# Layer 1 of an attention kernel: scores as three single-pass split products over four row tiles, with the work of a row redistributed and reordered

## What is computed

```python
bias = jnp.einsum('nijz,zh->nhij', pair_repr, bias_proj)[:, None]
gate = jax.nn.sigmoid(msa_repr @ gate_proj).reshape(bs, s, r, head, c)
q, k, v = jnp.split(msa_repr @ qkv_proj, 3, axis=-1)
...
sim = jnp.einsum('nsqhc,nskhc->nshqk', q, k) * scale
sim = jax.nn.softmax(sim, axis=-1)
sim = sim + bias
attend = jnp.einsum('nshqk,nskhc->nsqhc', sim, v) * gate
out = attend.reshape(bs, s, r, cm) @ out_proj
```

## Time and profile before

| | us |
|---|---|
| median of 3 runs (range) | 4940.08 (4938.53 to 4940.24) |
| the profiled execution | 4934.87 |
| its span, first to last instruction | 4932.9 |
| TensorE busy | 4651.9 |
| VectorE busy | 4024.4 |
| ScalarE busy | 3523.2 |
| GpSimd busy | 3464.3 |
| TensorE clock granted, mean | 0.973 of full |

### The profile page before, as it was taken

How to read it: one execution, slowest core, us unless ns; L and a number is a source line. 1 busy time by engine, 2 the same in 40 slices (tenths; PEclk the granted TensorE clock), 3 DMA queues, 4 the chain that set the end, 5 groups by cost and what they waited for, 6 DMA issues and landing times. The chain is left out here.

```text
span 4932.9 us, 149816 instructions
## 1 busy us (share of the span) xinstructions
PE 4651.9 (94%) x44087; PEld 3925.1 (80%) x44087; DVE 4024.4 (82%) x12910; ACT 3523.2 (71%) x11216; POOL 3464.3 (70%) x5926
## 2 busy tenths in 40 slices
PE   4663999999999999999999989999999999999999
PEld 2332888888888888888888868888888888888887
DVE  4445888888888988888888868888888888888887
ACT  2222888888888888888888866666666666666665
POOL 3332888888888888888888846666666666666665
PEclk8776999999999999999999989999999999999999
DMA  8995111111111111111111101111111111111111
GB/s 330 356 355 173 53 51 60 56 54 60 51 60 52 59 56 55 60 51 60 51 59 52 59 29 53 51 51 51 47 49 51 51 51 51 51 51 51 51 50 40
DMA packets 237352, 382.70 MB, mean 78 GB/s; under 512 B 18756, under 2 KB 156616, under 8 KB 224968
## 3 DMA queue, kind: packets, MB, share of 16 engines
q1 hardware_dynamic: 237256, 381.63, 23.0%
HBM read 309.21 MB, written 72.35 MB: 77 GB/s over the span
## 5 line engine op out<-in xcount | busy, mean ns | idle before, releaser
L1337 POOL TENSOR_SCALAR l_probs<-l_probs,l_inv 128x256 f32<-128x256 f32 x2048 | 943.2, 478 | 735.7 <-DVE l_inv L1242 730.2
L1161 ACT ACTIVATE l_probs<-bank,l_neg_max 128x256 f32<-128x256 f32 x2048 | 947.0, 481 | 486.2 <-DVE l_neg_max L1236 486.2
L563 POOL TENSOR_SCALAR l_probs<-l_probs,l_inv 128x256 f32<-128x256 f32 x2048 | 947.5, 476 | 279.6 <-DVE l_inv L814 279.6
L732 ACT ACTIVATE l_probs<-l_probs,l_neg_max 128x256 f32<-128x256 f32 x2048 | 1020.8, 518 | 10.3 <-DVE l_neg_max L806 10.0
L806 DVE CUSTOM_DVE_ANT_0 l_probs<-bank,bias 128x256 f32<-128x256 f32 x2048 | 779.6, 418 | 202.8 <-PE bank L673 199.1
L1236 DVE TENSOR_REDUCE l_neg_max<-bank 128x2 f32<-128x512 f32 x1024 | 646.6, 684 | 92.3 <-PE bank L1070 92.3
L1249 DVE TENSOR_TENSOR l_probs_t<-bank,bias 128x512 f32<-128x512 f32 x1024 | 674.6, 682 | 35.4 <-PE bank L1080 5.4
L673 PE MATMUL bank<-ident,l_probs 128*128 128x128 f32 x4096 | 629.5, 276 | 8.4 <-DVE l_probs_t L828 7.3
L1080 PE MATMUL bank<-ident,l_probs 128*128 128x128 f32 x4096 | 531.7, 273 | 3.2 <-POOL l_probs L1337 1.6
L673 PEld LDWEIGHTS bank<-ident,l_probs 128*128 128x128 f32 x4096 | 463.7, 141 | 44.7 <-issue 8.4
L686 PE MATMUL bank<-l_probs_t,l_v 128*64 128x256 f32 x4096 | 498.5, 385 | 0.2 <-issue 0.2
(11 more groups left out here) (196 smaller groups left out, 14011.6 us busy)
## 6 DMA issues: line engine op xcount, KB each, us to landing
fp_x<-in_x_dram SPq DMA_DIRECT2D x32, 1024.0 KB, 6.9
fp_ln_w<-in_L_conv_ln_w_dram SPq DMA_DIRECT2D x32, 1024.0 KB, 8.9
fp_ln_b<-in_L_conv_ln_b_dram SPq DMA_DIRECT2D x32, 1024.0 KB, 10.8
fp_pair<-in_L_conv_pair_repr_dram SPq DMA_DIRECT2D x32, 1024.0 KB, 13.4
l_x<-in_x_dram SPq DMA_DIRECT2D x128, 256.0 KB, 2.9
l_ln_w<-in_L_conv_ln_w_dram SPq DMA_DIRECT2D x128, 256.0 KB, 3.4
l_ln_b<-in_L_conv_ln_b_dram SPq DMA_DIRECT2D x128, 256.0 KB, 3.5
x<-l_y SPq DMA_DIRECT2D x128, 256.0 KB, 2.0
```

Source lines behind the costliest of these rows:

```text
L563: last = nc.gpsimd.tensor_scalar(probs[:, h, c], probs[:, h, c], inv[:, h, c:c + 1], 1.0, ALU.mult, ALU.mult)
L732: last = nc.scalar.activation(probs[:, h, c], probs[:, h, c], ACT.Exp, bias=neg_max[:, h, c:c + 1], scale=-1.0, accum_out=total[:, h, c:c ...
L1161: last = nc.scalar.activation(probs[:, h, c], b_s[h % 4][:, c * W:(c + 1) * W], ACT.Exp, bias=neg_max[:, h, c:c + 1], accum_out=total[:, h ...
L1337: last = nc.gpsimd.tensor_scalar(probs[:, h, c], probs[:, h, c], inv[:, h, c:c + 1], 1.0, ALU.mult, ALU.mult)
```

## The change

It touches `layer1` and the helper that writes out the loops.

- `scores` makes three single-pass products (high by high, high by low, low by high) for each head, 24 matmuls a quad in place of 8, accumulated in the same banks, on the same four row tiles.
- q and k are stored as high and low parts. ACT's copies make the high parts. `queries_low` on DVE reads q's bank again for the low part. For k, ACT copies the bank a second time (`keys_whole`), and `keys_low` on POOL subtracts.
- `group_norm` goes from DVE to ACT, as scale and bias by channel; the bias (-mean x 1/deviation) is made once ahead of the loop.
- `turn` runs five rows ahead (`AHEAD` 5, before 3), loads seven; quad 1's scores, half of the transposes and `attend` of a row come one step later than before. Every engine's order is new, and the bank hand-over waits of PE are written anew. `b_t` is chosen by the head's parity.
- The last two turns of each loop are written out (`ends=2`) instead of one.

The diff, cut to its core:

```diff
+    UNROLL, BUFS = 4, 4
+    AHEAD = 5
     QUADS = NH1 // 4
-    TURNS = (1, 0, 3, 2, 5, 4, 6, 7)
-    EXPS = (1, 2, 3, 0, 5, 4, 6, 7)
-    MAXIMA = (1, 2, 3, 0, 5, 4, 7, 6)
-    INVERSES = (1, 2, 3, 0, 5, 4, 6, 7)
-    DIVISIONS = (1, 3, 0, 2, 5, 4, 6, 7)
+    TURNS = (1, 2, 3, 0, 5, 4, 7, 6)
+    EXPS = (1, 2, 3, 0, 6, 5, 7, 4)
+    MAXIMA = (1, 2, 3, 0, 6, 7, 5, 4)
+    INVERSES = (1, 0, 2, 3, 6, 7, 5, 4)
+    DIVISIONS = (1, 2, 0, 3, 5, 4, 6, 7)
+    BIASED = (1, 2, 3, 0, 5, 4, 6, 7)
...
-        q = sb("q", [P, 2, HC, W])
-        kk_ = sb("k", [P, 2, HC, W])
+        q = [sb("q_high", [P, 2, HC, W], F32R), sb("q_low", [P, 2, HC, W], F32R)]
+        kk_ = [sb("k_high", [P, 2, HC, W], F32R), sb("k_low", [P, 2, HC, W], F32R)]
+        k_whole = sb("k_whole", [P, HC, W])
...
-            over_rows(engine, C0, UNROLL, row, ahead=AHEAD, behind=1)
+            over_rows(engine, C0, UNROLL, row, ahead=AHEAD, behind=1, ends=2)
...
-                if has(4):
-                    load(t, k + 4)
+                if has(7):
+                    load(t, k + 7)
...
             def turn(t, k):
-                s, i, tt = UNROLL * t + k, k % UNROLL, t + k // UNROLL
+                s, i, tt = UNROLL * t + k, k % BUFS, t + k // BUFS
                 pe.wait_ge(loaded[i], 16 * (tt + 1))
-                wait(pe, v_ready, s)
+                if exists(s - 3):
+                    pe.wait_ge(q_ready, s - 2)
+                elif exists(s - 4):
+                    pe.wait_ge(v_ready, s - 3)
+                elif exists(s - 1):
+                    pe.wait_ge(x_whole, s)
...
             def queries(t, k):
                 s = UNROLL * t + k
                 pe.wait_ge(x_ready, s + 1)
+                if exists(s - 1):
+                    pe.wait_ge(v_ready, s)
+                elif exists(s + 2):
+                    pe.wait_ge(x_whole, s + 3)
+                elif exists(s - 1):
+                    pe.wait_ge(q_ready, s)
...
             def keys(t, k):
                 s = UNROLL * t + k
                 pe.wait_ge(x_ready, s + 1)
-                if isinstance(s, int) and s < 3:
-                    wait(pe, g_ready, s)
-                    wait(pe, o_ready, s - 1)
-                else:
-                    pe.wait_ge(y_ready, s - 2)
+                if exists(s - 1):
+                    pe.wait_ge(g_ready, s)
+                elif exists(s - 3):
+                    pe.wait_ge(o_ready, s - 2)
+                elif exists(s - 4):
+                    pe.wait_ge(y_ready, s - 3)
+                elif exists(s - 1):
+                    pe.wait_ge(k_copied, s)
...
             def values(t, k):
                 s = UNROLL * t + k
-                pe.wait_ge(q_ready, s + 1)
+                pe.wait_ge(x_ready, s + 1)
+                if exists(s + 3):
+                    pe.wait_ge(x_whole, s + 4)
+                elif exists(s):
+                    pe.wait_ge(q_ready, s + 1)
+                elif exists(s - 1):
+                    pe.wait_ge(v_ready, s)
...
             def gates(t, k):
                 s = UNROLL * t + k
-                pe.wait_ge(k_ready, s + 1)
+                pe.wait_ge(x_ready, s + 1)
+                if exists(s - 2):
+                    pe.wait_ge(o_ready, s - 1)
+                elif exists(s - 3):
+                    pe.wait_ge(y_ready, s - 2)
+                elif exists(s):
+                    pe.wait_ge(k_copied, s + 1)
+                elif exists(s - 1):
+                    pe.wait_ge(g_ready, s)
...
                 for c in range(KC):
-                    for j in range(4):
-                        channels = slice(j * D1, (j + 1) * D1)
-                        last = nc.tensor.matmul(b_s[j][:, c * W:(c + 1) * W], q[channels, k % 2, quad, c * P:(c + 1) * P], kk_[channels, k % 2, quad],
-                                                start=True, stop=True, tile_position=(D1 * j, 0))
+                    for a, b in ((0, 0), (0, 1), (1, 0)):
+                        for j in range(4):
+                            channels = slice(j * D1, (j + 1) * D1)
+                            last = nc.tensor.matmul(b_s[j][:, c * W:(c + 1) * W], q[a][channels, k % 2, quad, c * P:(c + 1) * P],
+                                                    kk_[b][channels, k % 2, quad], start=a + b == 0, stop=a == 1, tile_position=(D1 * j, 0))
                 last.then_inc(s_mm[quad], 1)
 
...
             def transposes(t, k, h):
                 s = UNROLL * t + k
                 pe.wait_ge(p_ready, count(s, h, DIVISIONS))
-                wait(pe, t_ready, count(s, h, TURNS) - 2)
+                same = [g for g in TURNS if g % 2 == h % 2]
+                ahead = same[same.index(h) - 1]
+                wait(pe, t_ready, count(s if same.index(h) else s - 1, ahead, BIASED))
...
-                if inside(s + 1):
+                if exists(s - 1):
+                    pe.wait_ge(y_ready, s)
+                elif exists(s + 2):
+                    pe.wait_ge(k_copied, s + 3)
+                elif exists(s + 1):
                     pe.wait_ge(g_ready, s + 2)
-                else:
-                    pe.wait_ge(y_ready, s - 1)
+                elif exists(s - 1):
+                    pe.wait_ge(o_ready, s)
...
-                if inside(s + 1):
-                    pe.wait_ge(o_ready, s + 2)
-                else:
+                if exists(s + 3):
+                    pe.wait_ge(k_copied, s + 4)
+                elif exists(s + 2):
+                    pe.wait_ge(g_ready, s + 3)
+                elif exists(s):
+                    pe.wait_ge(o_ready, s + 1)
+                elif exists(s - 1):
                     pe.wait_ge(y_ready, s)
...
-                nc.scalar.activation(q[:, k % 2], b_xqv[:].rearrange("p (a c) -> p a c", a=HC), ACT.Copy).then_inc(q_ready, 1)
+                nc.scalar.activation(q[0][:, k % 2], b_xqv[:].rearrange("p (a c) -> p a c", a=HC), ACT.Copy).then_inc(q_high, 1)
...
-                nc.scalar.activation(kk_[:, k % 2], b_kgo[:].rearrange("p (a c) -> p a c", a=HC), ACT.Copy).then_inc(k_ready, 1)
+                nc.scalar.activation(kk_[0][:, k % 2], b_kgo[:].rearrange("p (a c) -> p a c", a=HC), ACT.Copy).then_inc(k_high, 1)
+
+            def keys_whole(t, k):
+                s = UNROLL * t + k
+                act.wait_ge(k_mm, s + 1)
+                wait(act, k_ready, s)
+                nc.scalar.activation(k_whole[:], b_kgo[:].rearrange("p (a c) -> p a c", a=HC), ACT.Copy).then_inc(k_copied, 1)
+
+            def group_norm(t, k):
+                s = UNROLL * t + k
+                act.wait_ge(x_mm, s + 1)
+                wait(act, x_ready, s - 1)
+                for c in range(HC):
+                    last = nc.scalar.activation(xf[:, k % 2, c], b_xqv[:, c * W:(c + 1) * W], ACT.Identity, bias=by_channel[:, 2, c:c + 1],
+                                                scale=by_channel[:, 1, c:c + 1])
+                last.then_inc(x_whole, 1)
...
-            def group_norm(t, k):
-                s = UNROLL * t + k
-                dve.wait_ge(x_mm, s + 1)
-                wait(dve, x_ready, s - 1)
-                for c in range(HC):
-                    last = nc.vector.tensor_scalar(xf[:, k % 2, c], b_xqv[:, c * W:(c + 1) * W], by_channel[:, 0, c:c + 1], by_channel[:, 1, c:c + 1],
-                                                   ALU.subtract, ALU.mult)
-                last.then_inc(x_whole, 1)
+            def queries_low(t, k):
+                dve.wait_ge(q_high, UNROLL * t + k + 1)
+                nc.vector.tensor_tensor(q[1][:, k % 2], b_xqv[:].rearrange("p (a c) -> p a c", a=HC), q[0][:, k % 2].bitcast(F32), ALU.subtract).then_inc(q_ready, 1)
...
+            nc.vector.scalar_tensor_tensor(out=by_channel[:, 2], in0=by_channel[:, 0], scalar=-1.0, in1=by_channel[:, 1],
+                                           op0=ALU.mult, op1=ALU.mult).then_inc(stat_ready, 1)
...
+            def keys_low(t, k):
+                pool.wait_ge(k_high, UNROLL * t + k + 1)
+                pool.wait_ge(k_copied, UNROLL * t + k + 1)
+                nc.gpsimd.tensor_tensor(kk_[1][:, k % 2], k_whole[:], kk_[0][:, k % 2].bitcast(F32), ALU.subtract).then_inc(k_ready, 1)
```

More of the change, by code:

```diff
@@ L42, in loop_first_peeled, with loop_ends_peeled @@
         body(t)
-def loop_ends_peeled(engine, count, body, hinted=None):
+def loop_ends_peeled(engine, count, body, hinted=None, ends=1):
     body(0, True, False)
-    with hinted.Fori(1, count - 1, engines=[engine.engine], hint_back_edge=True) if hinted else engine.Fori(1, count - 1) as t:
+    with hinted.Fori(1, count - ends, engines=[engine.engine], hint_back_edge=True) if hinted else engine.Fori(1, count - ends) as t:
         body(t, False, False)
-    body(count - 1, False, True)
+    for t in range(count - ends, count):
+        body(t, False, t == count - 1)
 def loop_stops_peeled(engine, count, stops, body, hinted):
@@ L63, in loop_stops_peeled, with over_rows @@
         done = stop + 1
```

(83 more changed lines are left out.)

131 lines of the change are left out of this document (68 added, 63 removed).

## The result

The changed kernel takes 4873.57 us (median of 4 runs, 4870.78 to 4877.42) against 4939.31 of the kernel before (4 runs): ratio 0.9868, 95% interval 0.9851 to 0.9885. The forecast was 4876 us, in a range of 4855 to 4915. The profiled execution took 4872.46 us with a span of 4870.7.

The account below looks back on a forecast made before the run. TensorE was taken to set the row time, 15.59 us. 125 rows at 15.05 save 67.5 us, the ends add 3: -64.5, 4870 on the profiled execution, plus 5.2 for the median, gives 4876 us, range 4855 to 4915.

Parts of the forecast that it names:

- The products: Layer 1 scores on TensorE: 24 single-pass matmuls take 0.90 us a quad instead of 1.07, saving 0.34 us per row.
- The order on TensorE: One row of layer 1, added up from old trace prices: 15.03 us, taken as 15.05, against 15.59 before.
- The K wait: TensorE's wait for the copy of K ahead of scores, 0.11 us a row, would be gone.
- The walk of slacks: One row walked through the engines' in-order queues: every wait of TensorE has positive slack, from 0.3 us up.
- The tightest place: Quad 1's scores waiting for head 0's exponents on ScalarE: slack 0.3 us, the smallest in the row.
- the gates: TensorE's gates, at 11.3 us in the walked row, wait for the output gated on VectorE: slack 0.4 us.
- The ends: Start and end of layer 1: start -2 to +2 us, end 31 to about 33 to 34; together +3.
- The sum: Whole kernel: 67.5 us less from 125 rows, 3 more at the ends, so -64.5 and 4876 us.
- Rival B: ScalarE 0.55 us later than walked, quad 1's scores wait about 0.25 us every row: 4907 us, chance 0.20.
- Rival C: Single-pass score groups do not overlap loads, step 0.21 us instead of 0.117: row 15.99, kernel 4993 us, chance 0.08.
- The rule of the Trainium skill: TensorE weight loads overlap matmuls in flight only when their row group differs; otherwise load and stream follow one another.

Follow-up runs that it names:

- experiment 1: Changed kernel with the eight fp32 score matmuls a quad of the kernel before put back, new order kept: 4916.96 us, ratio 0.9955.
- experiment 3: Changed kernel with the group norm put back on VectorE, new order kept: 4890.11 us, ratio 0.9900.
- experiment 10: Changed kernel with K's low part made on VectorE from the bank, without ScalarE's second copy and GpSimd's subtraction: 4874.49 us, ratio 0.9874.
- Experiment 2: Kernel before, in its old order, with the three single-pass score products and low parts of q and k on VectorE: 4986.88 us, ratio 1.0097.
- experiment 7: Changed kernel run once more, nothing altered: 4873.41 us, ratio 0.9874.
- Experiment 9: Changed kernel with the head as outermost loop of the scores, six matmuls of a head ahead of the next head's: 5140.85 us, ratio 1.0412.
- experiment 8: Changed kernel with loops over products and row tiles exchanged in the scores, three products of one head in a row: 4880.13 us, ratio 0.9880.

## Why the prediction was right

- *The products.* Forecast 0.34 us a row from two quads of 0.90; measured quads 0.91 and 0.92, and 0.34 in experiment 1. The step of 0.12 carries over from two row tiles to four.
- *The order on TensorE.* Forecast 15.03, taken as 15.05; measured 15.10 in one row and 15.085 in the mean. Item by item one row has keys 1.52, transposes 0.96, scores 0.92, turn and transposes 1.28, products 2.96, transpose 0.53, attend 1.86, scores 0.91, transpose 0.41, products 2.96, transposes 0.79. The two stretches of 24 products (2.96 for 2.94) and the scores (0.03 together) make the 0.07. The sum by prices of the trace before was good to 0.5%. Experiment 1 gives the order's own part as 0.17 us a row, forecast 0.22: 0.11 is the K wait, and of the rest the products take 0.25 less in one row of the trace after than before (7.44 for 7.69) and the transposes, the turn's among them and now in smaller groups, 0.19 more (3.97 for 3.78). No run separates the new order from the work moved between engines, but for the group norm (experiment 3) and K's low part (experiment 10).
- *The K wait.* Gone as forecast: 0.96 ahead of the scores. Experiment 2 shows the same wait grown by 0.74 when the low part is added without the reorder.
- *The walk of slacks.* The tightest place was named rightly and its slack of 0.3 measured as 0.34; the gates have 0.35 (walk: 0.4), `attend` 0.82 (0.9; 0.97 less the 0.15 at which it waits). Head 0's exponents end at 3803.2, 1.7 into the row (walk: 1.75); the group norm starts at 3805.58, 4.1 into it (4.1); the output is gated at 3811.66, 10.2 into it (10.1). One wait was missed: the values' copy has to wait for `attend` to free its buffer, so it starts at 3811.72, 10.2 into the row, and not at 8.9, where the walk has the exponents before it end. It cost nothing, since queries follow at 3814.36. In experiment 3 the same kind of walk named the wait for the residual rightly and saw a second one, for head 4's exponents, that came to 0.01. Timelines of ScalarE and VectorE:

```profile
3805.58 1.02 ACT L1242 ACTIVATE l_xf<-bank,l_by_channel 128x256 f32<-128x256 f32 x2 [0.76 <-PE bank L1030]
3811.72 0.60 ACT L1250 ACTIVATE l_v<-bank 128x512 f32<-128x512 f32 x1 [1.37 <-PE bank L1139]
3811.66 0.69 DVE L1325 SCALAR_TENSOR_TENSOR l_o<-l_gate,bank 128x512 f32<-128x512 f32 x1 [1.20 <-PE bank L1139]
```

- *The ends.* Forecast +3; measured -2.2 at the start and +3.1 at the end, +0.9. The start was the mis-sized term (-2 to +2 as a bound, zero taken). It is also the least certain: in experiment 7's trace of the same kernel it is -0.6.
- *The sum.* That the forecast came within 3 us is in part luck, three small errors of mixed sign. The row was 0.035 us longer, +4.4 over the layer; the ends were 2.1 less; and the median, taken as 5.2 above the profiled execution as it was before, lay only 1.1 above it (4873.57 against 4872.46), 4.1 less.
- *Rival B* did not happen, but it was close: 0.5 us more on ScalarE at that place costs 27 us, with 18% of ScalarE's time free.
- *Rival C* did not happen. A load takes 0.19 us and the groups follow each other every 0.12, so loads run beside the matmuls. (Ten steps of 0.093 more make 0.93 and not 0.96, which moves its 4993 by about 1 us.) Experiment 9 loses time in another way, with row tiles that do not work side by side; no run shows a step of 0.21.

## What to carry to other kernels

With one engine bound for the whole row, a reordered row can be priced by adding up start-to-start times of the old trace, changes of tile shape included. Busy times would not have given it: TensorE reads as busy for all of 1400 us with rows of 14.26, 15.09 and 17.16 us alike. What decides whether a cheaper operation is worth anything is the wait behind its new inputs: the same products cost 48 us in the old order and bring 43 in the new. A sum of free time on a helper engine says little; the slack is at one place in the row, and a spare instruction put there measures it. A short wait shows in no sum of idle time; it shows as a constant distance, row after row, between the end of what is waited for and the start behind it (here 0.15 us ahead of transposes, `attend` and gates, 0.29 to 0.31 ahead of scores).

## What the runs showed of the hardware

- The starts of matmuls on TensorE do not follow program order across row tiles. With three matmuls of one tile ahead of the next tile's, four tiles still start within one group (experiment 8: 0.93 us a quad, from 3807.63 to 3808.56); with six, the next tile starts only with the third (experiment 9: 1.94 us). The quad's time agrees with a tile that takes the matmul it starts and three more, beyond which the program's order holds the others back; that mechanism was not tested by itself, and no row shows where on the way from the kernel's text to the array the order changes.
- A weight load for the same row tile starts while that tile's matmul is in flight, with two tiles in layer 0, with four in the changed kernel and with one in experiment 9. The load takes 0.18 to 0.19 us and the single-pass step of 256 columns stays at 0.12. Timelines of the weight loads, of the changed kernel and of experiment 9, beside matmuls that start at 3803.97 and at 3814.02 (0.38 to 0.39 each):

```profile
3804.08 0.19 PEld L1107 LDWEIGHTS bank<-l_k_low,l_q_high 32*128 32x128 f32 x4
...
3814.12 0.18 PEld L1107 LDWEIGHTS bank<-l_k_low,l_q_high 32*128 32x128 f32 x1
```

  The rule of the Trainium skill that was weighed in the prediction (TensorE: Matmul & The Clock Gate, "What overlaps and what doesn't") does not hold here, nor does the strict order of matmuls that the same section states hold in experiments 8 and 9; the measurement decides.
- The granted clock was 1.00 (the 2.4 GHz level) through the steady stretch in both kernels, so it has no part in the difference.
